# A recurrent block and attention on one core: half of a causal convolution's taps as TensorE products

## The reference, cut to what matters

```python
xn = layernorm(x) * (1 + scale) + shift
x_in, z = split(xn @ in_proj_w.T)                 # 512 channels each
u = silu(causal_conv(x_in, conv_w, 4 taps) + conv_b)   # depthwise
dt_r, B, C = split(u @ x_proj_w.T)                # 64, 16, 16
dt = softplus(dt_r @ dt_proj_w.T + dt_proj_b)
h[t] = h[t-1] * exp(dt[t] * A) + dt[t] * u[t] * B[t]   # 512 channels x 16 states
y[t] = sum over states of h[t] * C[t]
out0 = x + gate * ((y + u * D_param) * silu(z)) @ out_proj_w.T
```

## Time and profile before

| | |
|---|---|
| median of 3 runs | 568.95 us (568.53 to 569.86) |
| the profiled execution | 569.01 us, its span 567.2 us |
| VectorE busy | 514.6 us (91%), 566 instructions |
| TensorE busy, products | 437.9 us (77%), 2456 instructions |
| GpSimd busy | 453.0 us (80%) |
| ScalarE busy | 408.6 us (72%) |
| mean granted clock of TensorE | 0.901 |

### The profile page before, as it was taken

The page is one execution under the profiler, slowest core; times in us unless marked ns, Lnnn a source line. Parts: engine busy times, 40 slices in busy tenths (PEclk is TensorE's granted clock), DMA queues, the critical chain, the costliest instruction groups (busy, mean ns, idle before and its releaser), DMA issues. The chain is left out here.

```text
span 567.2 us, 7391 instructions
## 1 busy us (share of the span) xinstructions
PE 437.9 (77%) x2456; PEld 361.2 (64%) x2456; DVE 514.6 (91%) x566; ACT 408.6 (72%) x897; POOL 453.0 (80%) x318
## 2 busy tenths in 40 slices
PE   8967666769789787768688678768787777866887
PEld 7646445657676676656576667647674666755776
DVE  2479899999999999999999999999999999999753
ACT  2693677668865998578966999488966988486533
POOL 4049969989998889979998889978997989985121
PEclk8988777896789798998989898998899898779899
DMA  9294032201430044001440045011440045000001
GB/s 269 66 326 125 3 114 85 102 4 54 159 112 0 29 151 154 14 19 40 159 131 1 28 151 165 2 29 43 147 129 1 10 151 166 2 0 20 0 1 37
DMA packets 22366, 45.38 MB, mean 80 GB/s; under 512 B 3685, under 2 KB 13557, under 8 KB 22329
## 3 DMA queue, kind: packets, MB, share of 16 engines
q1 hardware_dynamic: 22328, 44.92, 24.3%
HBM read 42.52 MB, written 2.39 MB: 79 GB/s over the span
## 5 line engine op out<-in xcount | busy, mean ns | idle before, releaser
L530 POOL TENSOR_TENSOR hs<-dtu,Br 128x1024 f32<-128x1024 f32 x127 | 297.0, 2362 | 8.5 <-DMA Br<-bc_rows 8.5
L722 ACT ACTIVATE ring<-dt,Aneg 128x256 f32<-128x256 f32 x512 | 212.9, 465 | 72.6 <-DVE hs L957 68.7
L950 DVE TENSOR_TENSOR_SCAN ring<-ring,hs 128x1024 f32<-128x1024 f32 x97 | 221.4, 2282 | 5.8 <-ACT ring L722 5.4
L1298 PE MATMUL sums<-ident,hs 128*128 128x128 f32 x1024 | 150.7, 303 | 36.3 <-DVE hs L957 36.0
L1298 PEld LDWEIGHTS sums<-ident,hs 128*128 128x128 f32 x1024 | 134.4, 158 | 48.3 <-DVE hs L957 44.7
L957 DVE TENSOR_TENSOR hs<-ring,Cr 128x1024 f32<-128x1024 f32 x97 | 118.8, 1225 | 3.3
L539 POOL TENSOR_TENSOR hs<-hs,Cr 128x1024 f32<-128x1024 f32 x31 | 73.2, 2360 | 42.1 <-DVE hs L950 42.1
L950 DVE TENSOR_TENSOR_SCAN hs<-ring,hs 128x1024 f32<-128x1024 f32 x31 | 70.3, 2269 | 0.0
L1366 PE MATMUL PY<-wqkvo,xT 128*128 128x256 f32 x168 | 46.6, 428 | 0.0
L1293 PE MATMUL sums<-ident,uD 128*128 128x128 f32 x64 | 15.5, 333 | 35.2 <-DVE ygT L964 35.2
L1366 PEld LDWEIGHTS PY<-wqkvo,xT 128*128 128x128 f32 x168 | 37.5, 223 | 6.6
(11 more groups left out here) (218 smaller groups left out, 694.1 us busy)
## 6 DMA issues: line engine op xcount, KB each, us to landing
Br<-bc_rows SPq DMA_DIRECT2D x32, 512.0 KB, 5.1
Cr<-bc_rows SPq DMA_DIRECT2D x32, 512.0 KB, 4.2
xg<-in_x SPq DMA_DIRECT2D x8, 256.0 KB, 2.9
out<-fin SPq DMA_DIRECT2D x7, 256.0 KB, 4.2
hs<-in_ada_wT SPq DMA_DIRECT2D x3, 512.0 KB, 4.6
win<-in_in_wT SPq DMA_DIRECT2D x2, 512.0 KB, 6.1
hs<-in_W_emb SPq DMA_DIRECT2D x2, 512.0 KB
gate<-gate_rows SPq DMA_DIRECT2D x8, 128.0 KB, 3.1
```

Of the source, the lines that this page charges most:

```text
L530: nc.gpsimd.tensor_tensor(hs[:, g % DBUF], dtu[:, b % 2, dc, :].unsqueeze(1).to_broadcast([P, NQ, T]), Br[:, NQ * q:NQ * q + NQ, :], ALU.m ...
L722: ins = nc.scalar.activation(ring[:, g % 2, j, :], dt[:, b % 2, dc, :], ACT.Exp, scale=Aneg[:, c:c + 1])
L950: V.tensor_tensor_scan(driven if by_pool(g) else decays, decays, driven, 0.0, ALU.mult, ALU.add).then_inc(s_scan_done, 1)
L1298: ins = M(YT[:, c, :], hs[:, g % DBUF, j, P * c:P * c + P], ident[:, :], is_transpose=True, start=False, stop=(q == UPC - 1 and j == NQ - ...
```

## The change

From batch 2 on the second half of x_in (256 channels, h = 1, two blocks of 128) is no longer projected and then filtered. Its four taps are folded into the weights: for each tap s a copy of the in_proj columns times the channel's tap weight, applied to `xnT` shifted by s steps, all summed in PSUM. The first half, z, and batches 0 and 1 are computed as before.

- TensorE: `taps_of_block` in place of `in_proj(b, 1)`: per block 4 taps x 2 parts of D; the first block in slot -16, the second in slot -15. `in_proj_2` moves from slot -14 to -13, `in_proj_3` from -13 to -12 (batch 1 stays). What they wait for is the same read of `PX`; for a folded half that is ScalarE's copy alone.
- ScalarE: `conv_last_tap_1` moves from slot -14 to -12 (batch 1 stays), and its scale is 1 for a folded half.
- VectorE: `conv_taps(b, 1)` returns at once.
- GpSimd: three products of 128x512 in the start (`scale_taps`, g = -6) write the weights of taps 1 to 3, one at g = 14 (`scale_last_tap`) scales `win` itself by the last tap's weights, once batch 1 has used it.
- SP: two loads more, the tap rows in broadcast to all partitions (384 KB and 128 KB), behind W_emb and ahead of `broadcast_bc(0)`. They land in buffers not yet in use.

```diff
+FOLDED = (1,)
+FOLD_LO, FOLD_N = 2 * P * FOLDED[0], 2 * P * len(FOLDED)
+def folded(b, h):
+    return b >= 2 and h in FOLDED
+def taps_until(b, h):
+    return sum(3 * 2 for c in range(b + 1) for k in range(2) if not folded(c, k) and (c, k) <= (b, h))
...
+            sp.dma_start(wrow, a["tap_rows"][1:TAPS, FOLD_LO:FOLD_LO + FOLD_N].unsqueeze(0).to_broadcast([P, TAPS - 1, FOLD_N])).then_inc(
+                s_ld_taps, 16)
+            sp.dma_start(last_row, a["tap_rows"][0, FOLD_LO:FOLD_LO + FOLD_N].unsqueeze(0).to_broadcast([P, FOLD_N])).then_inc(
+                s_ld_taps, 16)
             broadcast_bc(0)
...
+            def scale_taps():
+                pool.wait_ge(s_ld_taps, 32)
+                pool.wait_ge(s_ld_win, 16)
+                for s in range(1, TAPS):
+                    nc.gpsimd.tensor_tensor(wtap[:, s - 1], win[:, :, FOLD_LO:FOLD_LO + FOLD_N],
+                                            wrow[:, s - 1, :].unsqueeze(1).to_broadcast([P, KD, FOLD_N]), ALU.mult).then_inc(s_taps_ready, 1)
+                pool.wait_ge(s_taps_ready, TAPS - 1)
+            def scale_last_tap():
+                pool.wait_ge(s_xz_mm, 4 + 2)
...
             for g in range(FIRST, LAST):
+                if g == -6:
+                    scale_taps()
+                if g == 14:
+                    scale_last_tap()
...
+                    tap = 1.0 if folded(b, h) else pcol("conv_w", TAPS * dc + 3, TAPS * dc + 4)
                     nc.scalar.activation(conv[:, dc, :], xz_bank(b, h)[:, e, :], ACT.Identity, bias=pcol("conv_b", dc, dc + 1),
-                                         scale=pcol("conv_w", TAPS * dc + 3, TAPS * dc + 4)).then_inc(s_conv0_ready, 1)
+                                         scale=tap).then_inc(s_conv0_ready, 1)
...
             def silu_u(b):
-                act.wait_ge(s_tap_done, 3 * DC * (b + 1))
+                act.wait_ge(s_conv0_ready, DC * (b + 1))
+                act.wait_ge(s_tap_done, taps_until(b, 1))
...
-                for slot, step in ((-17, normalize0), (-16, modulated), (-15, conv_last_tap_0), (-14, conv_last_tap_1),
+                for slot, step in ((-17, normalize0), (-16, modulated), (-15, conv_last_tap_0), (-12, conv_last_tap_1),
...
             def conv_taps(b, h):
+                if folded(b, h):
+                    return
...
+            def wait_x_read(b, h):
+                pe.wait_ge(s_conv0_ready, DC * b + 2 * h + 2)
+                if not folded(b, h):
+                    pe.wait_ge(s_tap_done, taps_until(b, h))
...
+            def taps_of_block(b, h, e):
+                if e == 0:
+                    wait_x_read(b, h - 1)
+                    if b == 2:
+                        pe.wait_ge(s_taps_ready, TAPS)
+                lo = P * (2 * h + e)
+                for s in range(TAPS):
+                    for k in range(KD):
+                        w = wtap[:, s - 1, k, lo - FOLD_LO:lo - FOLD_LO + P] if s else win[:, k, lo:lo + P]
+                        ins = M(PX[:, e, s:T], w, xnT[:, k, 0:T - s], start=(s == 0 and k == 0),
+                                stop=(s == TAPS - 1 and k == KD - 1), skip_group_check=True)
+                if e == 1:
+                    ins.then_inc(s_xz_mm, 1)
...
-                for slot, step in ((17, transpose_back), (-19, transpose_x), (-18, in_proj_0), (-16, in_proj_1), (-14, in_proj_2),
-                                   (-13, in_proj_3), (39, output), (-9, x_proj), (-8, dt_proj_0), (-6, dt_proj_1),
+                for slot, step in ((17, transpose_back), (-19, transpose_x), (-18, in_proj_0), (-16, in_proj_1),
+                                   (-15, in_proj_1b), (-13, in_proj_2), (-12, in_proj_3), (39, output), (-9, x_proj), (-8, dt_proj_0), (-6, dt_proj_1),
...
-                    b = due_by(g, slot, -2 if step is in_proj_1 else 2 if step in (in_proj_2, in_proj_3) else 0)
+                    b = due_by(g, slot, -2 if step is in_proj_1 else 1 if step in (in_proj_2, in_proj_3) else 0)
```

More of the change, by code:

```diff
@@ L154, in build @@
         conv = sb("conv", [P, DC, T])
+        wtap = sb("wtap", [P, TAPS - 1, KD, FOLD_N])
         vln = conv
@@ L189, in build @@
         PZ = ps("PZ", [P, 2, T])
+        wrow = hs[:, 1, 1:NQ, :]
+        last_row = fin[:, 0, :]
         staged = hs[:, 5:10].rearrange("p s n t -> p (s n t)")
@@ L204, in build @@
         s_ld_post = sem("ld_post")
+        s_ld_taps = sem("ld_taps")
+        s_taps_ready = sem("taps_ready")
         s_pool_const = sem("pool_const")
@@ L554, in rstd2 @@
                 rstd(s_st2_ready, b, mv2, ve2, rs2, nb2, s_ve2_ready, s_rs2_ready, s_nbp2)
+            def scale_taps():
[7 more added lines that the diff above has]
+                pool.wait_ge(s_xz_mm, 4 + 2)
+                part = win[:, :, FOLD_LO:FOLD_LO + FOLD_N]
+                nc.gpsimd.tensor_tensor(part, part, last_row.unsqueeze(1).to_broadcast([P, KD, FOLD_N]),
+                                        ALU.mult).then_inc(s_taps_ready, 1)
             for g in range(FIRST, LAST):
+                if g == -6:
+                    scale_taps()
+                if g == 14:
+                    scale_last_tap()
                 if 0 <= g < NB * U:
@@ L874, in _ @@
                                    (33, copy_kT), (38, normalize2), (42, finish)):
-                    late = 2 if step in (conv_last_tap_0, conv_last_tap_1) else 1 if step is modulated else 0
+                    late = 2 if step is conv_last_tap_0 else 1 if step is modulated else 0
                     b = due_soon(g, slot) if step is normalize0 else due_by(g, slot, late)
@@ L913, in conv_taps @@
                         if s > 1:
-                            dve.wait_ge(s_tap_done, 3 * DC * b + 6 * h + 2 * (s - 2) + e + 1)
+                            dve.wait_ge(s_tap_done, taps_until(b, h) - 6 + 2 * (s - 2) + e + 1)
                         w = pcol("conv_w", TAPS * dc + 3 - s, TAPS * dc + 4 - s)
@@ L1232, in in_proj @@
                     if h >= 2:
-                        pe.wait_ge(s_tap_done, 3 * DC * b + 6 * (h - 1))
+                        wait_x_read(b, h - 2)
                 elif h <= 2:
-                    pe.wait_ge(s_tap_done, 3 * DC * b + 6 * h)
+                    wait_x_read(b, h - 1)
                 else:
@@ L1525, in in_proj_1, with in_proj_1b @@
             def in_proj_1(b):
-                in_proj(b, 1)
+                if folded(b, 1):
+                    taps_of_block(b, 1, 0)
+                else:
+                    in_proj(b, 1)
+            def in_proj_1b(b):
+                if folded(b, 1):
+                    taps_of_block(b, 1, 1)
             def in_proj_2(b):
@@ L1595 @@
         "ada_b": L0_cond_ada_b, "in_wT": np.asarray(L0_cond_in_proj_w).T, "xp_wT": np.asarray(L0_cond_x_proj_w).T,
+        "tap_rows": np.asarray(L0_cond_conv_w).reshape(DI, TAPS).T[::-1],
         "dt_wT": np.asarray(L0_cond_dt_proj_w).T, "dt_b": L0_cond_dt_proj_b, "out_wT": np.asarray(L0_cond_out_proj_w).T, "Wq": L1_cond_Wq,
```

## The result

The changed kernel took **594.55 us**, median of 4 runs (593.48 to 594.68), against 569.4 (568.53 to 571.23, 4 runs) of the kernel before beside it: a ratio of 1.0434 (95% interval 1.0410 to 1.0458). It is 25 us slower. The profiled execution took 594.47 us, its span 592.7, at a mean granted clock of 0.891.

A forecast was written before the change was run, and what follows sets the result against it. VectorE, 91% busy, was taken to bound the kernel, but delayed TensorE sums and ScalarE decays outweigh its saved taps: 2.0 + 2 x 5.1 + 3 x 3.9 = 23.9 us on 569.0 gives 593 us, range 578 to 604.

The forecast's parts named there:

- Removed: VectorE's six tap instructions in each of batches 2 to 7: 2.34 us a batch, 14.0 us in all.
- Added: TensorE's two tap blocks of 3.46 us replace four products of 1.73: 5.2 us more a batch, 31 in all.
- First meeting: VectorE's gate in unit 4 needs TensorE's sum of unit 3: slack of 1.4 us becomes a 3.3 us wait.
- S: End of TensorE's sum of unit 3, forecast 14.1 us behind X, at 311.4 in batch 4.
- X: Start of TensorE's first block of taps in unit 0, forecast unchanged at 297.26 in batch 4.
- Second meeting: VectorE's scan of unit 8 needs ScalarE's decays: forecast at S + 16.2, 5.1 us later in batch 4.
- Waits for sums: Sign in VectorE's waits: for sums from 1.2 us to some 16, for decays from 5 to some 25.
- Moved copy, GpSimd, SP's loads: Side terms at 0 each; bounds 1.3 us for GpSimd, 2 for the loads; uncovered, the copy costs 1.0 a batch.
- TensorE hides the blocks: Rival: the chain to the sum of unit 3 ends within 14.3 us, taps' gain is kept, 555 us; chance 0.11.
- only the gate matters: Rival: ScalarE's queue has missed slack, only the gate of unit 4 waits, 2.8 us in all, 572; chance 0.08.
- X's clock: TensorE's level ahead of the first block: high in batches 3, 5, 6 (3.9 us later), otherwise 5.1 later.
- the clock behind the gap: TensorE behind in_proj_2: transposes and sum low, in_proj_3 high; high throughout S + 14.5 (584), low throughout S + 18 (602).

The follow-up runs named there:

- experiment 5: The kernel before plus only the change's two loads and four GpSimd products, results unused: 569.91 us, ratio 1.0019.
- experiment 1: The changed kernel with the sum of unit 3 ahead of out_proj in TensorE's queue: 594.18 us, ratio 1.0453 against the kernel before.
- experiment 6: 30 useless products in TensorE's gap ahead of transpose_y: in the changed kernel 576.06 us; 18 such products in the kernel before: 570.08 us.
- experiment 2: The changed kernel with z's products back in slots -14 and -13: 576.36 us; companion with in_proj_3 alone moved to -13: 576.54 us.
- experiment 3: The kernel before with only z's two products moved to slots -13 and -12: 578.87 us, ratio 1.0161.
- experiment 4: The changed kernel with taps 2 and 3 of the folded half left out: 575.49 us, ratio 1.0117 against the kernel before.
- experiment 7: The changed kernel with both repairs, z's products in their old slots and the sum of unit 3 ahead of out_proj: 562.63 us, ratio 0.9878.

## Why the prediction was right

Forecast 593.0, measured 594.55, inside 578 to 604. By its steps:

- *Removed:* 14.0 us forecast, 13.7 measured. Added: a block is 310.24 - 306.80 = 3.44 us (3.46).
- *First meeting:* S = X + 14.0 (14.1); the gate waits 3.6 us (3.3).
- *Second meeting:* unit 8's scan at S + 16.0 (16.2), through `copy_z` at S + 1.75, `transpose_y` at S + 5.4 and `silu_z_second` at S + 10.6, forecast at 1.9, 5.5 and 10.8. Waits for sums 21.2 us (16), for decays 24.8 (25).
- *Moved copy, GpSimd, SP's loads:* 0 forecast. ScalarE waited 1.23 us for the second block in its moved copy, but the decays that follow it were done long before their scan; the start is bounded by experiment 5.
- *Rivals:* that TensorE hides the blocks would have needed the gate without a wait, and it waits in every batch. That only the gate matters is refuted by experiment 1. What held was the order of the queues; in experiment 6 TensorE had more work and the kernel was faster.

**The term that was mis-sized is the clock's, and the sum was luckier than its parts.** I took X's clock from the kernel before: low in batches 2 and 4, high in 3, 5 and 6, hence 5.1, 3.9, 5.1, 3.9 and 3.9. It was low in 3 to 6 and high in 2. Unit 8's scans, VectorE's timeline, batches 1, 2, 3 and 5:

```profile
133.42 2.27 DVE L994 TENSOR_TENSOR_SCAN ring<-ring,hs 128x1024 f32<-128x1024 f32 x1
...
200.08 2.30 DVE L994 TENSOR_TENSOR_SCAN ring<-ring,hs 128x1024 f32<-128x1024 f32 x1 [3.21 <-ACT ring L765]
...
268.48 2.30 DVE L994 TENSOR_TENSOR_SCAN ring<-ring,hs 128x1024 f32<-128x1024 f32 x1 [3.22 <-ACT ring L765]
...
405.13 2.30 DVE L994 TENSOR_TENSOR_SCAN ring<-ring,hs 128x1024 f32<-128x1024 f32 x1 [3.21 <-ACT ring L765]
```

With 336.81 in batch 4 and 473.42 in batch 6, and the same scans of the kernel before (195.70, 258.74 and 449.07 in batches 2, 3 and 6), the delays added from batch to batch are 1.4, 3.0, 5.4, 4.6, 5.3 and 4.8 us for batches 1 to 6, together 24.4 against the forecast 23.9. Batches 3, 5 and 6 cost more than forecast, 1, 2 and 4 less. Another 1.1 us, for which I had nothing, are two longer waits in the last batch, for the attention products' input (1.49 us against 0.72) and at the last gate (1.58 against 1.23).

Nor did the clock behind the gap go as I took it. The four transposes and the sum behind them had 0.69 and in_proj_3 0.64, where I had low, then high; the two errors cancel to 0.2 us. By the rule of the Trainium skill that the prediction weighed (TensorE: Matmul & The Clock Gate, Part 4: PE-mode transpose: transposes do not engage the full clock) in_proj_3 runs low behind them; here it began low and ended high (a granted 0.50 until 330.4, then 1.00), so it fits the rule in part. The four transposes ahead of it do not, any more than the earlier trace rows do: they ran at 1.00. By the rule the end was S + 18, and it was S + 16.0. My range gave a high clock 5 x 1.7 = 8.5 us. At the second meeting it was worth just that, 8.4 (experiment 6), but some 16 in all, since it acts at the next batch's first meeting as well. Both expectations of experiment 2 missed by the same omission.

**Left open:** why a gap ahead of `transpose_y` goes with a low level at attention products more than 40 us later, with much work between. In the four kernels with a gap of 3.7 to 3.8 us there (the changed one and those of experiments 1, 3 and 4) the attention products ran low in batches 3 to 6 every time, 16 of 16. In the eight others that can be compared, with a gap of 2.4 us or less, a filled one or none, they did so in 5 of 32. So with a shorter gap the low level was rare, but not ruled out: with both repairs there is no gap, and in batch 6 the attention products still ran at 0.54 and the first block came 3.74 us behind them:

```profile
414.04 1.84 PE L1493 MATMUL PY<-att,qT 128*128 128x128 f32 x8 [0.70 <-DVE att L1046]
...
417.78 1.03 PE L1313 MATMUL PX<-xnT,win 128*128 128x256 f32 x4
```

That batch 2 is spared in the changed kernel says nothing of the gap: `transpose_y` first runs in unit 3 of batch 2, behind these attention products, and they ran low there in other kernels (the kernel before, and those of experiments 3 and 7).

## What to carry to other kernels

Before work is moved onto an idle engine, write down its queue around the next place where someone waits for it: a fifth to a quarter of idle time hid none of the added work at this place, while one swap in the queue and one slot for z's products were worth 32 us with the same instructions. If one delay feeds two meetings, repairing one alone can show nothing (0.4 us here, and 14 once the other was repaired); take the repairs together before judging a change. A gap on TensorE ahead of a product on the path is priced by the level it leaves behind as well as by its length.

## What was not expected of the hardware

- Behind a gap of 3.7 us on TensorE the products began fast and then slowed (in_proj_3 2.87 us against 1.88), and in four of five batches the attention products of the next batch ran at 0.53 or 0.54. With the gap filled by 30 small bf16 products (3.44 us) all of batch 4, from its attention products to 10 us behind in_proj_3, ran at 1.00.
- The fall did not come in the idle time but behind it. In batch 4 the granted clock was 1.00 through the gap and the four transposes (to 326.8; 0.66 us, as fast as behind a filled gap), 0.50 from 327.2 to 330.4, and 1.00 again behind that. The eight sum instructions in the fall took 1.77 us, and take 1.04 at the high level.
